# A two-layer graph network on one core: TensorE signals once for several pieces of its work, and older sums are issued ahead of products

## What is computed

```python
# layer 0
msg = relu(x[src] + edge_attr);  agg = segment_sum(msg, dst)
h = x + (x + agg);  f = gelu(bn1(h) @ W1.T + b1) @ W2.T + b2
x1 = layernorm(x + bn2(h + f))
# layer 1
h = gelu((x1[src] + edge_attr) @ W1m + b1m)
agg = segment_sum(h @ W2m + b2m, dst) / max(degree, 1)
u = gelu(agg @ W1u + b1u) @ W2u + b2u
out = layernorm(x1 + layer_norm(x1 + u, gamma, beta))
```

## Time and profile before

| | |
|---|---|
| time, median of 3 runs | 2640.95 us (2634.74 to 2650.4) |
| profiled execution, span from the first instruction to the last | 2670.8 us |
| TensorE matmuls busy | 2066.5 us (77%), x9234 |
| VectorE busy | 1471.0 us (55%) |
| ScalarE busy | 1309.5 us (49%) |
| GpSimd busy | 1639.4 us (61%), 1663 of its 1689 instructions being gathers |
| HBM | 499.54 MB read, 66.49 MB written, 212 GB/s over the span |

### The profile page before, as it was taken

One profiled execution on the slowest core, in us unless ns is written; L12 is line 12 of the kernel. 1 busy time (PEld: TensorE's weight loads), 2 busy tenths in 40 slices (PEclk: granted clock), 3 DMA queues, 4 the chain that ended last, 5 costly groups with the idle time before them and its releaser, 6 DMA issues.

```text
span 2670.8 us, 37695 instructions
## 1 busy us (share of the span) xinstructions
PE 2066.5 (77%) x9234; PEld 1690.3 (63%) x9234; DVE 1471.0 (55%) x3208; ACT 1309.5 (49%) x2691; POOL 1639.4 (61%) x1689
## 2 busy tenths in 40 slices
PE   4787777777777787887657888788788788878878
PEld 3566666666566566666446666666676666666766
DVE  3355555454554544545435665666666566666666
ACT  4555455554555554555324454454454454444453
POOL 6666666666666666664366666666666566666650
PEclk9898988889989888889868888898988988988897
DMA  6788778878788788887446666666666666666661
GB/s 215 247 268 258 257 257 258 271 248 275 252 263 265 252 262 264 261 264 248 146 144 174 180 184 179 178 191 179 180 186 181 177 178 178 189 182 177 186 187 49
DMA packets 347352, 566.93 MB, mean 212 GB/s; under 512 B 48104, under 2 KB 213604, under 8 KB 347284
## 3 DMA queue, kind: packets, MB, share of 16 engines
q1 hardware_dynamic: 267098, 347.29, 42.1%
q0 software_dynamic: 79824, 218.08, 26.9%
q10 hardware_dynamic: 362, 0.85, 0.1%
HBM read 499.54 MB, written 66.49 MB: 212 GB/s over the span
## 4 chain that ended last, share of the span: by engine, by line
PE 29%; another core or an unknown queue 23%; issue 19%; DVE 13%; ACT 11%; DVEq 4%; ACTq 1%; DMA 0%; POOL 0%; POOLq 0%; SPq 0%
PE bank L1051 11%; PE bank L993 5%; DVE m_lo L1312 3%; PE bank L1018 3%; ACT bank L735 3%; ACT m_all L739 3%; PE bank L1068 3%; PE bank L963 2%; DVEq L1265 2%; PE bank L890 2%; DVE sel L1246 1%; PE bank L975 1%; DVE bank L1306 1%; ACT bank L768 1%
## 5 line engine op out<-in xcount | busy, mean ns | idle before, releaser
L564 POOL DMA_INDIRECT m_all<-y_scratch,src_u x831 | 808.4, 973 | 492.4 <-DVE bank L1306 259.9
L564 POOL DMA_INDIRECT m_all<-in_x,src_p x816 | 807.0, 989 | 417.0 <-issue 210.8
L1051 PE MATMUL bank<-w1m_sb,e_all 128*128 128x256 f32 x2076 | 607.4, 437 | 221.7 <-DVE m_lo L1312 125.7
L1051 PEld LDWEIGHTS bank<-w1m_sb,e_all 128*128 128x128 f32 x2076 | 425.2, 217 | 312.8 <-issue 129.4
L993 PE MATMUL bank<-m_all,sel 128*128 128x257 f32 x1664 | 496.1, 430 | 138.7 <-ACT m_all L739 110.0
L1306 DVE TENSOR_TENSOR bank<-bank,m_all 128x512 f32<-128x512 f32 x416 | 289.8, 697 | 454.6 <-remote 306.8
L993 PEld LDWEIGHTS bank<-m_all,sel 128*128 128x128 f32 x1664 | 345.7, 214 | 240.2 <-ACT m_all L739 125.8
L1018 PE MATMUL bank<-w1m_sb,ez 128*128 128x256 f32 x1248 | 357.1, 412 | 141.6 <-issue 74.8
L767 ACT ACTIVATE m_hi<-bank 128x512 fp32r<-128x512 f32 x416 | 248.3, 597 | 320.4 <-DVE bank L1306 112.2
L1018 PEld LDWEIGHTS bank<-w1m_sb,ez 128*128 128x128 f32 x1248 | 242.7, 204 | 191.7 <-issue 162.3
L1068 PE MATMUL bank<-m_lo,sel 128*128 128x256 f32 x831 | 302.4, 385 | 36.9 <-issue 24.1
(11 more groups left out here) (176 smaller groups left out, 2063.0 us busy)
## 6 DMA issues: line engine op xcount, KB each, us to landing
e_all<-in_edge SPq DMA_DIRECT2D x416, 256.0 KB
e_all<-in_edgeT SPq DMA_DIRECT2D x208, 256.0 KB
ez<-in_edgeT SPq DMA_DIRECT2D x104, 384.0 KB
z_scratch<-zc SPq DMA_DIRECT2D x104, 384.0 KB
e_all<-z_scratch SPq DMA_DIRECT2D x104, 256.0 KB
e_all<-in_edgeT SPq DMA_DIRECT2D x104, 128.0 KB
e_all<-z_scratch SPq DMA_DIRECT2D x104, 128.0 KB
m_all<-y_scratch,src_u POOLq DMA_INDIRECT x831
```

Of the source, the lines that this page charges most:

```text
L564: pool.indirect_dma_start(out=m_sb[n % ROUND][:, t, :], out_offset=None, in_=table, in_offset=bass.IndirectOffsetOnAxis(ap=sources(g, u), ...
L1051: last = pe.matmul(z_bank(s)[:, t * D:(t + 1) * D], eT_sb[s % ERING][:, k, t * P:(t + 1) * P], w1m_sb[:, k, :], start=(k == 0), stop=(k == ...
```

## The change

TensorE's increments are taken away where a later one can stand for them, and the waits are put on the later one:

- First pass: `z_ahead0`, `z_ahead` and (but for the last group) `sum_turned` are gone. `pair_summed` is raised by 2 at j = 1, on the last matmul of the turned sum, and by 2 at j = 3. The product a = 1 moves from j = 2 to j = 1.
- Second pass: `pair_summed` is raised by 4 once per group; `sum_turned` only for the last 7 groups. `sums_split` of the pair four back is issued ahead of `product`, so that a product's `z_made` also tells that those sums are done. ScalarE's gelu therefore waits for `pair_summed` at j = 3 alone, and VectorE's accumulation waits for a `z_made` instead of `sum_turned`.
- `copy_sums` loses its wait for `sum_turned`.

```diff
@@ SyncE, edges_first
-                    sp.wait_ge(z_ahead, g)
+                    sp.wait_ge(pair_summed, PAIRS * g)
@@ ScalarE
             def keep_two(i, q):
-                act.wait_ge(z_ahead0, PER_ROUND * i + q + 1)
+                g = PER_ROUND * i + q
+                act.wait_ge(pair_summed, PAIRS * g + (PAIRS if known(g) and g == G - 1 else 2))
             def keep_third(i, q):
-                act.wait_ge(z_ahead, PER_ROUND * i + q + 1)
+                g = PER_ROUND * i + q
+                act.wait_ge(pair_summed, PAIRS * g + (2 if known(g) and g == G - 1 else PAIRS))
             def gelu(i, s):
                 act.wait_ge(added, M + ROUND * i + s + 1)
-                if not (known(i) and ROUND * i + s < ZBANKS):
+                if s % PAIRS == 3 and not (known(i) and ROUND * i + s < ZBANKS):
                     act.wait_ge(pair_summed, M + ROUND * i + s - ZBANKS + 1)
             def copy_sums(first, i, q):
                 act.wait_ge(pair_summed, first + PAIRS * h + PAIRS)
-                if not (known(h) and first == 0 and h < 2):
-                    act.wait_ge(sum_turned, first // PAIRS + h - 1)
@@ TensorE
             def ahead(i, q, a):
-                if a:
-                    last.then_inc(z_ahead if a == AHEAD - 1 else z_ahead0, 1)
             def sums(i, s):
-                last.then_inc(pair_summed, 1)
+                return last
             def turn_group(first, i, q):
-                turn_sums(bank[2 if first else q % 2], sum_n[q % 2], first == 0).then_inc(sum_turned, 1)
+                return turn_sums(bank[2 if first else q % 2], sum_n[q % 2], first == 0)
             def sums_split(i, s):
-                last.then_inc(pair_summed, 1)
+                if j == 3:
+                    last.then_inc(pair_summed, PAIRS)
             def first_pass(i, s):
                 q, j = divmod(s, PAIRS)
+                before = (i, q - 1) if q else (i - 1, PER_ROUND - 1)
                 if not known(i) or i * ROUND + s < M:
-                    if known(i) and PER_ROUND * i + q == G - 1:
-
-                        if j < 3:
-                            ahead(i, q, (0, 2, 1)[j])
-                    elif j != 1:
-                        ahead(i, q, max(j - 1, 0))
-                    sums(i, s)
-                before = (i, q - 1) if q else (i - 1, PER_ROUND - 1)
-                if j == 1 and (not known(i) or 0 <= PER_ROUND * before[0] + before[1] < G - 1):
-                    turn_group(0, *before)
+                    a = (0, 2, 1, None)[j] if known(i) and PER_ROUND * i + q == G - 1 else (0, 1, None, 2)[j]
+                    if a is not None:
+                        ahead(i, q, a)
+                    last = sums(i, s)
+                    if j == 1 and (not known(i) or PER_ROUND * i + q > 0):
+                        last = turn_group(0, *before)
+                    if j % 2:
+                        last.then_inc(pair_summed, 2)
                 if known(i) and i * ROUND + s == M:
-                    turn_group(0, *before)
+                    turn_group(0, *before).then_inc(sum_turned, 1)
             def second_pass(i, s):
                 q, j = divmod(s, PAIRS)
-                if j < 3 and (not known(i) or i * ROUND + s < M):
-                    product(i, s, act_low)
                 earlier = (i, s - 4) if s >= 4 else (i - 1, s - 4 + ROUND)
                 if not known(i) or 0 <= ROUND * earlier[0] + earlier[1] < M:
                     sums_split(*earlier)
+                if j < 3 and (not known(i) or i * ROUND + s < M):
+                    product(i, s, act_low)
                 if last_group(TURNS, i, s):
-                    turn_group(G, *last_group(TURNS, i, s))
+                    turn_group(G, *last_group(TURNS, i, s)).then_inc(sum_turned, 1)
@@ VectorE, accumulate_group
-                dve.wait_ge(sum_turned, h + 1)
+                if known(g) and first == 0 and g == G - 1:
+                    dve.wait_ge(sum_turned, 1)
+                elif known(g) and first and g >= G - LAST_SUMS:
+                    dve.wait_ge(sum_turned, 2 + g - (G - LAST_SUMS))
+                elif first:
+                    dve.wait_ge(z_made, 3 * (g + 3) + 2)
+                else:
+                    dve.wait_ge(pair_summed, PAIRS * (g + 1) + 2)
```

More of the change, by code:

```diff
@@ L333, in build @@
         ez_in, z_out = sems("ez_in", 2), sems("z_out", 2)
-        z_ahead0, z_ahead, z_kept0, z_kept, z_put = map(sem, ("z_ahead0", "z_ahead", "z_kept0", "z_kept", "z_put"))
+        z_kept0, z_kept, z_put = map(sem, ("z_kept0", "z_kept", "z_put"))
         e_moved = sem("e_moved")
@@ L1017, in ahead @@
                 for k in range(KD):
-                    last = pe.matmul(ahead_bank[a // 2][:, a % 2 * D:(a % 2 + 1) * D],
-                                     ez_sb[q % 2][:, k, a * P:(a + 1) * P],
-                                     w1m_sb[:, k, :], start=(k == 0), stop=(k == KD - 1))
-                if a:
-                    last.then_inc(z_ahead if a == AHEAD - 1 else z_ahead0, 1)
+                    pe.matmul(ahead_bank[a // 2][:, a % 2 * D:(a % 2 + 1) * D],
+                              ez_sb[q % 2][:, k, a * P:(a + 1) * P],
+                              w1m_sb[:, k, :], start=(k == 0), stop=(k == KD - 1))
             def sums(i, s):
```

## The result

The changed kernel takes **2633.0 us**, median of 12 runs (2625.8 to 2637.56); the kernel before, run beside it as often, 2640.66 us (2633.91 to 2650.4). The ratio is 0.9967, 95% interval 0.9953 to 0.998: some 8 us, 0.3%. The forecast was 2536 us, and of its three outcomes the one that came, within 0.5%, had the chance 0.13. Rival 1, "the number doesn't matter", had given 2650 us. The stated range, 2400 to 2655 us, holds 2633 us only at its upper end, which was there for rivals 1 and 4; the likeliest case's own range, 2437 to 2620, does not.

The account below looks back on a forecast made before the run. No engine was taken as full; TensorE's signals, delivered late in bursts while GpSimd gathers, were taken to bound the kernel. -113 - 9 + 16 = -106 us, 4.0%, applied to the 2641 us median gave 2536 us, range 2400 to 2655.

Parts of the forecast that it names:

- three outcomes: Whole kernel: faster by more than about 0.5%, chance 0.78; within 0.5%, 0.13; slower, 0.09.
- Rival 1: A run of gathers holds back all TensorE signals until it ends, whatever their number; about 2650 us, chance 0.10.
- rivals 1 and 4: The fourth: a signal costs TensorE only its own writing, late bursts have another cause; about 2648 us, chance 0.03.
- the likeliest case: Both passes: loss from late TensorE signals shrinks with their number; 2536 us, own range 2437 to 2620, chance 0.66.
- Part 4: Waits removed or replaced on ScalarE and VectorE (gelu, accumulation): 0 us each, nothing new queued behind them.
- Part 1: Fewer TensorE signals, 61% less in the first pass, 46% in the second: -113 us, and -9 us at the second pass's start.
- trickle in order: While gathers run, single TensorE signals get through in order, so a needed one stands behind others; read from a 20.47 us wait.
- None is full: Windows view of both passes: no engine is full, TensorE has some 20% to spare, so waits decide.
- rival 3: The signal backlog dissolves, pauses vanish, and GpSimd's 1.25 us a gather bounds: about 2300 us, chance 0.12.
- Part 5: Second pass, sums ahead of products: each product ends 0.66 us later; +16 us, 206 us at most.
- rival 2: Second pass: later products at j = 0 become the uncovered bound, 69 us; 2710 us, chance 0.09.
- Parts 2 and 3: First pass: product a = 1 moved to j = 1; coarser slot signals. 0 us each; uncovered, 90 us and 300 us.

Follow-up runs that it names:

- e10: Kernel before with only the second pass's new order (sums ahead of products), all signals kept, and half the gathers left out: 1877.57 us, ratio 0.8494.
- e13: Kernel before with all its gathers, each fetching 64 rows instead of 128: 2145.97 us against 2209.99, ratio 0.972.
- e1: Kernel before with only the first pass's part of the change: 2651.82 us against 2658.0, ratio 0.9978.
- e2: Kernel before with only the second pass's part of the change: 2660.69 us against 2658.0, ratio 1.0007.
- e3: Changed kernel with 3536 added signals that nobody waits for: 2656.75 us against the kernel before at 2658.0, ratio 1.0003.
- e9: Kernel before with a ninth gather per group, of half rows into a buffer nobody reads: 2935.14 us against 2644.87, ratio 1.1097.
- e5: Kernel before with only the second pass's order changed (sums ahead of products), all signals kept: 2659.98 us against 2658.0, ratio 1.0002.
- e11: Kernel before with only the first pass's part of the change and half the gathers left out: 1873.33 us, ratio 0.8483 to the kernel before.
- e15: The unchanged kernel run once more for a second trace, on the fourth chip: 2628.0 us, a single run.
- e8: Kernel before with as many gathered rows of half the length, 512 B instead of 1 KB: 2659.59 us against 2644.87, ratio 1.0052.
- e12: Kernel before with only the second pass's part of the change and half the gathers left out: 1876.19 us, ratio 0.8488 to the kernel before.

## Why the prediction was wrong

**What held.** TensorE's signals are late, in bursts, and only while GpSimd gathers: with half of the gathers the unknown queue falls from 23% to 1% of the chain. On the chip of e10 to e13 they are not late at all. No wait was hidden in the code that I had missed; Part 4's "0 us each" fits e1 and e2.

**The step that failed** is in Part 1: "what follows if the loss shrinks as the signals do", from which came -113 us. I had two ends, nothing and 390 us, and took a value between them by a proportion that no row supported. The row that spoke against it was in my own text: "the burst comes when GpSimd pauses". A burst that waits for a pause has a time of its own that the number of signals does not enter. The "trickle in order" that I set against it rested on one wait, and that wait was still there after the change, 26.0 us long. Nearly four times the removed signals, added back, cost 9.5 us (e3), and the whole change is worth some 8 us where Part 1 alone had been put at 113 and 9. **Rival 1 is what happened.**

**A second step failed in the reading of GpSimd.** I took "8 x 1.25 = 10.0 us" as its work and the rest of the 12 us as its pause, so time to be won (163 and 227 us). e9 shows that a further gather costs 1.40 us. At that price eight are 11.2 of the 11.8 us of a first-pass group; by the bursts, 1.45 to 1.46 each, even 11.6. 1663 gathers at 1.40 us are 2328 of the 2641 us. So most of the pauses was not time that fewer signals could win. The first section's "None is full" misled: GpSimd, 61% busy by the page, sets the time. And at that price rival 3, bounded "by GpSimd's 1.25 us a gather", was out of reach on these chips.

What fills the pauses stays open. I read them as the end of the gathers' own work, which the rows do not show; they can as well be a hold that outlasts the run and keeps a freed slot from being told. e9 fits both. Against the first, taken alone, stands the start of the second pass: from 1302.91 GpSimd begins 44 gathers, one every 1.26 us, and the last of them is this one in the timeline of the kernel before:

```profile
1357.00 0.94 POOL L564 DMA_INDIRECT m_all<-y_scratch,src_u  x1 [0.31 <-issue]
```

**Part 5.** +16 us was priced as if TensorE's order mattered under the gathers; e5 measured 1.0002. Uncovered, the same edit costs 2.1% of the second pass (e10 and e11), some 16 us in 750, or 1.3% on the other chips: the size was near and the cover was missed. Its form then is rival 2's, a later product that returns as a later low part, and not the occasional wait of VectorE that I priced. Under the gathers, which set a group's time, it did not show.

**Parts 2 and 3.** 0 us holds, under cover: e1 is no slower but 0.2% faster. Their cover was named as TensorE's idle time and slots filled ahead; with TensorE full (e11) they cost 2.3% of the first pass, some 17 us in 750, far less than my "90 us" and "300 us".

**Where the 8 us come from.** They come with the first pass (e1: 0.9978). A slot is told free for two pairs at once, so GpSimd gathers in fewer and longer runs, 98 stops for 128, and each stop may cost it the way of a signal to it. That is only argued: nothing was run that joins the gathers and leaves the signals as they were. In e15, an execution of the unchanged kernel as quick as the changed one, there are still 115 stops (64 to remote and 51 to L993), so the number of stops alone does not set the time.

**On the other side** the change costs 1.6% as soon as the gathers are no longer the bound. No version that beats both kernels came out of these runs. Whoever wants one has to start with the gathers: with half of them the time is 29% less, with TensorE at 96%.

## What to carry to other kernels

An engine that is 61% busy can set the time: add one more of its instructions per turn and see what the kernel pays (here 1.40 us for 1.25 shown), before its pauses are read as time to be won. When a wait ends late and nothing in the trace ended with it, ask which other engine's run of work ended just then, and count the time from the start of that run, before the number of messages is blamed. And cover is not only a reason to price an edit at nothing; an edit that pays nothing under it may cost something when the cover goes, so measure it with the bound taken away too.

## What the runs showed of the hardware

- On three chips, while GpSimd issues indirect gathers of 128 rows, many signals of TensorE to the other engines are held, often to 1.43 to 1.46 us for each gather from the start of the run (8 gathers: 11.6 us; 9 gathers: 13.2 us). In those two bursts ScalarE, VectorE and GpSimd get them within 0.3 us of each other. On the chip of e10 to e13 no wait is put to "remote". Why TensorE's signals, and what holds them, no run shows; nor does a count of gathers explain the long wait at the start of the second pass.
- An indirect gather's row shows 0.95 us and 0.30 to the next; a ninth one in each group costs 1.40 us (e9), and 512 B a row instead of 1 KB change nothing (e8: 1.0052).
- A semaphore increment on each matmul of `ahead` does not lengthen the step of 216 ns from one to the next (e3), and 3536 more increments cost the kernel 9.5 us. The changed kernel raises `pair_summed` by 2 and by 4 at once.
- Chips differ, above all where gathers are the pace: 2644 to 2658 us on three of them and 2210 us on the other for the same kernel. With half of the gathers the unchanged kernel took 1876 and 1878 us on two of the three, and the near variants e10 to e12 1873 to 1878 us on the other. 2210 us for 1663 gathers bounds one there at 1.33 us, under the 1.40 measured elsewhere. That chip was used in one series alone (e10 to e13), so what makes it differ stays open. What the change is worth there was not run.
